# Transposing h inside the previous tile's down product, in a routed feed-forward kernel

## What is computed

```python
x = x + jnp.tanh(g_xattn[0]) * _L0_xattn_ref(_layernorm(x), ctx_1024, Wq, bq, Wk, bk, Wv, bv)   # 8 x 256 tokens of 256
# feed-forward, I = 704, E = 8, on hidden_states = layernorm(x)
routing_indices = jnp.argmax(router_logits, axis=-1)
for e in range(E):
    mask = (routing_indices == e)[..., None]
    xe = jnp.where(mask, hidden_states, 0.0)
    g = jnp.einsum('sbh,ih->sbi', xe, gate_w[e])
    u = jnp.einsum('sbh,ih->sbi', xe, up_w[e])
    ye = jnp.einsum('sbi,hi->sbh', jax.nn.silu(g) * u, down_w[e])
    out = out + jnp.where(mask, ye, 0.0)
# x + tanh(g_ffn[0]) * out
```

## Time and profile before

| | before |
|---|---|
| median of 3 runs | 236.29 us (235.4 to 236.63) |
| the profiled execution | 235.78 us |
| its span in the profile | 233.9 us |
| PE busy | 199.9 us, 85% of the span |
| DVE, ACT, POOL busy | 132.8, 107.5, 133.0 us |
| L860, up product | 360 matmuls, 83.2 us |
| L872 and L875, down product | 220 matmuls, 42.9 and 28.0 us |
| L839, transposes of h | 120, 16.5 us |

### The profile page before, as it was taken

How to read it: one execution, slowest core, us unless ns; L and a number is a source line. 1 busy time by engine, 2 the same in 40 slices (tenths; PEclk the granted TensorE clock), 3 DMA queues, 4 the chain that set the end, 5 groups by cost and what they waited for, 6 DMA issues and landing times.

```text
span 233.9 us, 4473 instructions
## 1 busy us (share of the span) xinstructions
PE 199.9 (85%) x1187; PEld 171.1 (73%) x1187; DVE 132.8 (57%) x436; ACT 107.5 (46%) x217; POOL 133.0 (57%) x124
## 2 busy tenths in 40 slices
PE   0797699998774788999999999999999999999620
PEld 0655688896674667888887888888888887888510
DVE  0289689977669505636544636546546545556410
ACT  2233577776420145465339475267494304443200
POOL 3000009869273699329966989967989962331110
PEclk9999999999859559999999999999999999999985
DMA  4999211773910116641481093381011031110010
GB/s 83 369 382 383 98 48 46 245 271 116 372 36 0 55 38 244 213 152 45 144 326 28 1 353 115 137 323 49 1 49 44 1 93 24 49 46 4 1 45 0
DMA packets 11824, 29.41 MB, mean 126 GB/s; under 512 B 2222, under 2 KB 8241, under 8 KB 10770
## 3 DMA queue, kind: packets, MB, share of 16 engines
q1 hardware_dynamic: 6848, 21.70, 26.1%
q0 software_dynamic: 2064, 5.12, 7.3%
q10 hardware_dynamic: 2882, 2.24, 2.8%
HBM read 24.85 MB, written 4.72 MB: 126 GB/s over the span
## 4 chain that ended last, share of the span: by engine, by line
PE 72%; DVE 13%; issue 5%; DMA 4%; ACT 2%; SPq 1%; POOL 0%; ACTq 0%; POOLq 0%; DVEq 0%
PE ps L860 33%; PE ps L872 12%; PE ps L839 6%; PE ps L875 5%; DMA xin<-in_x 4%; PE ps L746 3%; PE ps L767 3%; DVE st L942 2%; PE ps L717 2%; PE ps L832 2%; PE ps L728 2%; PE ps L756 2%; PE ps L708 1%; PE ps L809 1%; DVE V L1067 1%
## 5 line engine op out<-in xcount | busy, mean ns | idle before, releaser
L860 PE MATMUL ps<-wgu,xhT 128*128 x360 | 83.2, 385 | 1.2 <-issue 1.2
L860 PEld LDWEIGHTS ps<-wgu,xhT 128*128 128x128 f32 x360 | 66.4, 192 | 12.4 <-issue 1.6
L872 PE MATMUL ps<-wd,hT 128*128 x120 | 42.9, 395 | 2.5 <-DVE hT L1112 2.4
L451 POOL DMA_INDIRECT xin<-x_rows,table x23 | 22.8, 990 | 31.7 <-DVE xin L1133 22.8
L386 POOL TENSOR_TENSOR wgu<-raw_gu,wgu (+1 forms) x12 | 38.6, 3252 | 0.1
L1120 DVE TENSOR_TENSOR A<-xin,ps 128x512 f32<-128x512 f32 (+1 forms) x40 | 20.5, 520 | 26.7 <-ACT xin L624 12.2
L409 POOL TENSOR_TENSOR wgu<-raw_gu,wgu 128x352 fp32r<-128x352 f32 x16 | 14.5, 945 | 34.7 <-ACT wgu L548 34.7
L624 ACT ACTIVATE xin<-ps 128x512 f32<-128x512 f32 (+1 forms) x40 | 18.4, 466 | 31.5 <-PE ps L860 27.8
L456 POOL DMA_INDIRECT out<-xin,table x20 | 20.3, 1016 | 19.7 <-DVE xin L1133 14.5
L618 ACT ACTIVATE hT<-ps 128x512 fp32r<-128x512 f32 x20 | 11.9, 593 | 35.3 <-PE ps L839 30.9
L875 PE MATMUL ps<-wd,hT 128*128 x100 | 28.0, 280 | 0.0
(11 more groups left out here) (148 smaller groups left out, 290.2 us busy)
## 6 DMA issues: line engine op xcount, KB each, us to landing
raw_gu<-in_Wgu SPq DMA_DIRECT2D x8, 1408.0 KB, 8.1
both<-in_Wd SPq DMA_DIRECT2D x8, 640.0 KB, 4.6
xin<-in_x SPq DMA_DIRECT2D x8, 256.0 KB, 8.0
x_rows<-x ACTq DMA_DIRECT2D x8, 256.0 KB, 4.2
both<-in_WdL SPq DMA_DIRECT2D x16, 64.0 KB, 4.7
both<-in_ctxT SPq DMA_DIRECT2D x1, 960.0 KB, 8.2
xin<-x_rows,table POOLq DMA_INDIRECT x23
out<-xin,table POOLq DMA_INDIRECT x20
```

The source lines that it names most:

```text
L451: pool.indirect_dma_start(out=xg[:, j % SEATS, :], out_offset=None, in_=rows, in_offset=bass.IndirectOffsetOnAxis(ap=table[:, j:j + 1], ax ...
L860: last = pe.matmul(ps[:, g, 0:2 * WIDE if g < 2 else 4 * REST], xhT[:, j % 2, x_part, c, :], w, start=(c == 0 and (x_part, w_part) == (0, 0)),
L872: last = pe.matmul(ps[:, 6, 0:2 * H], hT[:, 0, c, :], wd[:, slot, c].rearrange("p o a n -> p (o a n)"), start=(c == 0), stop=(c == CI - 1) ...
```

## The change

The six transposes of h of tile j+1 move into `down(j)`, behind its fourth chunk. With the stagger, round j now does `turn_x(j+1)`, `up(j)`, and `down(j-1)` with the transposes of h of tile j between chunks 3 and 4. In round 0, which has no down product, they stand at its end. The last down product, in `drain`, has none. Streams of other engines are as they were; ACT's and DVE's waits too. In the changed file, L872 and L875 are L876 and L879.

```diff
-            def down(j):
+            BEFORE_TURN = 4
+
+            def down(j, turn=True):
...
                 for c in range(CI):
+                    if turn and c == BEFORE_TURN:
+                        turn_h(j + 1)
                     last = pe.matmul(ps[:, 6, 0:2 * H], hT[:, 0, c, :], wd[:, slot, c].rearrange("p o a n -> p (o a n)"),
...
             def tile(j, first=False, ahead1=True, ahead2=True):
                 know(j)
                 if j > SURE:
                     know(j - 1)
-                if not first:
-                    turn_h(j - 1)
                 if first:
                     up(j)
                 if ahead1:
                     turn_x(j + 1)
-                if not first:
+                if first:
+                    turn_h(j)
+                else:
                     up(j)
                     down(j - 1)
 
             def drain(j):
                 if j >= SURE:
                     know(j)
-                turn_h(j)
-                down(j)
+                down(j, turn=False)
```

## The result

| | before | after |
|---|---|---|
| median | 236.44 us (235.4 to 236.63, 4 runs) | 241.27 us (240.24 to 242.78, 4 runs) |
| the profiled execution | 235.78 us | 240.88 us |
| its span | 233.9 us | 239.1 us |

The changed kernel is slower: the ratio is 1.022, with a 95% interval of 1.015 to 1.028. The prediction was 240.0 us, 238.3 to 241.8, and 0.87 for slower.

What follows compares the result with a forecast made beforehand. PE was taken to bound the tiles. Terms 0.3+0.2+0.4+2.2+0.5+0.4 = 4.0 us gave 239.8 on the profiled 235.78 and 240.3 on the median 236.29; forecast 240.0 us, range 238.3 to 241.8.

Steps and rivals of the forecast that it cites:

- The step on which all hung: On PE, the sequencer doesn't pass transposes waiting for v_h, so expert loads and branches behind them are given out later.
- the first rival: PE's sequencer runs ahead past the waiting transposes, so loads and branches cost nothing: 237.2 or 236.7 us; chance 0.12.
- ordinary rounds: Rounds 1 to 15: sequencer reaches up at D+2.70, PE wants it at D+2.91 (D: down's first weights load); cost nil.
- head of round 1: No down product stands in front and the expert's load now follows the transposes, so up starts later: +0.3 us.
- 15 to 16 and 16 to 17: Reading the number of tiles, a branch and expert loads delay up: +0.2, then +0.4 us; +0.6 in all.
- 17 to 18 and 18 to 19: The sequencer's way of 2.1 us now follows the wait, delaying up: +1.1 us each, +2.2, the largest term.
- rounds with a late h: Where h comes late PE stands still longer: +0.5 us in round 8, 0 in round 5; 0 to 1 in another execution.
- the end: finish(18) on DVE also waits for six transposes and delays turned_h(19), holding the last down product: +0.4 us.
- The hold that was to be absorbed: Round 16's down product already waited 0.43 us for its hT, so 0.43 of up(16)'s 0.59 delay is absorbed.
- The clock: Holes of 1.1 us drop TensorE from 2.4 to 1.2 GHz; one round at half speed costs 6.7 us, 246.7; chance 0.03.
- The second rival: Ordinary rounds lack the margin, h or up 0.1 to 0.3 us late in each: 241.4 to 244.2 us; chance 0.15.
- "Faster": Next tile's transposes are done 0.6 us earlier, which could let hT come sooner where ACT is late; chance 0.02.

Runs made afterwards that it cites:

- one pair held: Changed kernel with the next expert's load in rounds 1 to 14 put behind the first of the six transposes; 248.24 us in one run.
- Early loads: Changed kernel with reads of experts and number of tiles moved ahead of the wait for h: 237.14 us, 1.007; same loads in the kernel before: 236.08 us, 1.006.
- doubled loads: Changed kernel with the tile's expert read twice in rounds 1 to 15; 247.72 us, ratio 1.056.
- three chunks: Changed kernel with the transposes of h behind three chunks of the down product instead of four; 245.62 us, ratio 1.048.
- DVE reordered: Changed kernel with DVE's finish of a tile moved behind turned_h of the next tile; 247.3 us.
- added matmuls: 24 unread matmuls ahead of the last down product: in the changed kernel 241.67 us, 1.029; in the kernel before with experts read early 236.56 us, 1.004.

## Why the prediction was right

**The mechanism.** The step on which all hung was that the sequencer doesn't pass the transposes before v_h has come. It holds: in round 4 the load of the expert moved from 1.1 us ahead of the down product to 0.36 behind h. It is 0.07 behind h where no chunk stands between, 0.32 with two, 0.44 with three, and 0.05 with one pair held. Early loads take the cost away, and doubled loads add to it. The prediction had asked for a load within 0.3 of h; with two chunks it is just outside, 0.32 to 0.41 in the rounds 1 to 14. The last L1111 stands right behind `finish(18)`, as it was to.

The Trainium skill (Perfetto Trace Analysis, Per-engine timelines, Tensor Engine Instruction) says that an instruction is pushed into a wait queue and the sequencer is then ready for the next one; the run with one pair behind the wait doesn't agree for a weight load that waits for h, so the first rival falls.

**The terms**, each from starts of loads in the two profiles:

| step | predicted | measured | from |
|---|---|---|---|
| ordinary rounds | 0 | 0.0 | D+2.92 against D+2.91 |
| head of round 1 | +0.3 | +0.43 | 91.10-89.82 = 1.28 against 0.85 |
| 15 to 16 and 16 to 17 | +0.6 | +0.92 | +0.77, +0.59, less the 0.44 of hold absorbed |
| 17 to 18 and 18 to 19 | +2.2 | +2.16 | D+4.05 and D+3.93 against D+2.91 |
| rounds with a late h | +0.5 | about +0.2 | what is left of 4.2 |
| the end | +0.4 | +0.48 | 5.49 against 5.01 from D to the last down |
| sum | 4.0 | 4.2 | the stretches |

The hold that was to be absorbed in round 16 was: PE has no idle time there ahead of down. The way through the branches was put 0.2 us too short in round 15: D+3.68 where D+3.50 was worked out (D+3.52 in the second profile). In round 16 it was put 0.15 too short, D+4.05 for D+3.90.

**What the sum lacked.** On the profiled executions the difference is 5.1 us (240.88 less 235.78). Beyond the 4.2 there are 1.4 for the last down product at the lower clock, 0.2 for a later start of the tiles, and -0.6 behind the last down. The clock was a rival with 0.03, and worked out as a whole round at half speed. It came in a smaller form, at the end, where the prediction had the kernel before at full speed behind 2.06 us of idling and took it to stay so. The half speed that it read off "at the beginning" lies in the sort and the first tile (0.54 from 64 to 70 us, 0.53 from 76 to 82). It isn't shown that the low clock at the end comes with the change. The changed kernel's two profiles have it (3.09 and 2.66 us); the kernels with doubled loads, with three chunks and with DVE reordered don't (1.73). Leaving out the runs with added matmuls, none of three profiles with the transposes at the old place has it, and six of nine with them moved have some of it.

**Late h.** The size of this term was small in this pair because the late rounds differ from execution to execution: in both profiles they came to about 1.2 to 1.4 us. That this term and that of the rounds 15 to 17 were off in opposite directions is luck, and brings the sum nearer to 4.2 than its parts are. The step was right that a late h costs more at the new place: up in round 8 came at D+3.33 where it had been D+2.90. With three chunks it was worth 4.3 us in one profile.

**The second rival**, that the margin of ordinary rounds isn't there, falls at four chunks and is true at three. The margins of 0.16 and 0.2 us were real, and as small as they had been said to be. **"Faster"** had nothing for it.

The time itself, 241.27, is 1.3 above the forecast and inside the range, and 1.4 of the profiled difference is the clock at the end, which the forecast had at nothing. The second measurement of the change, 5.9 above the kernel before on its chip, says that the forecast's 3.7 to 4 was low rather than high.

## What to carry to other kernels

When an instruction that waits is moved up in a stream, list what the engine's sequencer has to do behind it: register loads, branches, address arithmetic. They were free as long as the sequencer was ahead, and they stop being free once they take longer than the work that the engine still has behind the wait. Read these values a round or more ahead; and before reordering an engine's queue, ask who waits for the moved instruction, and not only what stands behind it.

## What was not expected of the hardware

**ACT starts late beside indirect DMAs.** In some rounds the second silu starts 0.2 to 1.9 us later than in the others. This is round 8 of the changed kernel on ACT and, in the last rows, POOL's gathers and scatters at that time:

```profile
143.06 0.33 ACT L624 ACTIVATE xin<-ps 128x192 f32<-128x192 f32 x1 [0.89 <-issue]
...
139.97 1.02 POOL L456 DMA_INDIRECT out<-xin,table  x1 [0.30 <-issue]
141.29 0.97 POOL L451 DMA_INDIRECT xin<-x_rows,table  x1 [0.30 <-issue]
142.57 1.01 POOL L456 DMA_INDIRECT out<-xin,table  x1 [0.30 <-issue]
```

D is 142.17 there; in ordinary rounds this silu starts at D+0.37, here at D+0.89. No row shows anything that it waits for ("issue"). The rounds are 2, 5, 8, 10 and 13, and in two profiles 15, most of them only in some executions. In round 8 it is 0.3 to 1.9 late in every profile with all scatters (but that with DVE reordered, where the rounds lie otherwise), and in none of the two without twelve of them. In round 5, where the scatters were kept, it stays late. That they belong together is likely from this, and what the link is stays open.

**TensorE's clock at the end of an idle stretch** isn't decided by its length in these profiles. The changed kernel's last down product stood behind 2.85 us of idling and ran at the lower level. That of the kernel with the transposes behind all six chunks did so (0.54 of full speed, 2.99 us from first to last load) behind 2.29, as much as the kernel before had, whose clock was 1.00. That of the kernel with doubled loads had 2.85 and ran at full speed, and that of the kernel with DVE reordered ran so behind 3.59. The first loads of these three:

```profile
223.78 0.19 PEld L874 LDWEIGHTS ps<-wd,hT 128*128 128x128 f32 x1 [2.29 <-issue]
```

```profile
231.60 0.19 PEld L876 LDWEIGHTS ps<-wd,hT 128*128 128x128 f32 x1 [2.85 <-issue]
```

```profile
233.11 0.19 PEld L876 LDWEIGHTS ps<-wd,hT 128*128 128x128 f32 x1 [3.59 <-issue]
```

**Reading a value from SBUF into a register** takes PE's sequencer 0.65 us in round 4 of the kernel with doubled loads, of which 0.30 is the load.
